# A decoder layer with routed experts: the places of rows in the experts' regions summed by PE, base sums in a buffer of their own, and another order of small parts

## The reference, cut to what matters

```python
x = LN(x + attention(x))            # 8 heads, q/k 64 wide, v 16 wide, relative bias
x = LN(x + mlstm(x, ctx, ctx))      # 4 heads of 32, input and forget gates, decay matrix, running maxima
x = LN(x + ffn(x))

def ffn(x):                                     # H=128, F=512, one shared expert, 8 routed, 2 chosen
    shared = gelu(x @ shared_up) @ shared_down
    probs = softmax(x @ router_w)               # 8 columns
    p, idx = top_k(probs, 2)
    routed = sum over the two chosen e of p_e * (gelu(x @ up[e]) @ down[e])
    return shared + routed + x
```

## Time and profile before

| | us |
|---|---|
| three runs | 477.38, 479.07, 479.12 |
| median | 479.07 |
| profiled execution, its time | 479.12 |
| profiled execution, its span | 477.3 |
| PE busy | 451.4 (95%) |
| PE weight loads busy | 381.6 (80%) |
| DVE busy | 314.0 (66%) |
| ACT busy | 278.6 (58%) |
| POOL busy | 185.4 (39%) |
| mean granted clock of PE | 0.982 |

### The profile page before, as it was taken

One profiled execution on the slowest core, in us unless ns is written; L12 is line 12 of the kernel. 1 busy time (PEld: TensorE's weight loads), 2 busy tenths in 40 slices (PEclk: granted clock), 3 DMA queues, 4 the chain that ended last, 5 costly groups with the idle time before them and its releaser, 6 DMA issues.

```text
span 477.3 us, 15261 instructions
## 1 busy us (share of the span) xinstructions
PE 451.4 (95%) x5178; PEld 381.6 (80%) x5179; DVE 314.0 (66%) x1020; ACT 278.6 (58%) x626; POOL 185.4 (39%) x207
## 2 busy tenths in 40 slices
PE   8899999999988999898799999999999999999994
PEld 6588888888877777666567999999999999999731
DVE  5477888888887478888966666445454444445255
ACT  5678777867685989868768853132233333333236
POOL 5872022102000111117766656477655555554400
PEclk9999999999999999989987999999999999999998
DMA  5341424900000052012211212323222222222196
GB/s 143 87 130 52 103 53 109 237 3 1 3 25 23 25 206 61 25 45 69 63 57 58 74 38 65 90 79 87 75 71 68 66 66 66 66 66 63 47 313 203
DMA packets 47880, 37.98 MB, mean 80 GB/s; under 512 B 5456, under 2 KB 41184, under 8 KB 47824
## 3 DMA queue, kind: packets, MB, share of 16 engines
q1 hardware_dynamic: 43072, 28.10, 21.8%
q0 software_dynamic: 4320, 8.92, 5.2%
q10 hardware_dynamic: 432, 0.20, 0.1%
HBM read 19.30 MB, written 16.34 MB: 75 GB/s over the span
## 4 chain that ended last, share of the span: by engine, by line
PE 59%; DVE 21%; ACT 10%; issue 4%; DMA 4%; DVEq 1%; SPq 0%; POOL 0%; ACTq 0%; POOLq 0%
PE bank L1284 14%; PE bank L1274 14%; PE bank L1234 6%; DMA wdn<-routed 3%; PE bank L966 2%; PE bank L913 2%; PE bank L956 2%; PE bank L915 2%; PE bank L914 2%; DVE negmax L1406 2%; DVE prob L1403 2%; PE pair L1266 2%; DVE tkr L1397 2%; DVE cmat L1504 1%; PE pair L936 1%
## 5 line engine op out<-in xcount | busy, mean ns | idle before, releaser
L853 ACT ACTIVATE prob<-bank 128x512 f32<-128x512 f32 x71 | 42.4, 597 | 104.9 <-PE bank L1274 103.1
L535 POOL DMA_INDIRECT routed<-zbuf x71 | 73.9, 1040 | 59.2 <-DVE zbuf L1763 46.6
L1284 PE MATMUL bank<-wdn,prob 128*128 x568 | 78.2, 281 | 0.2 <-issue 0.2
L1274 PE MATMUL bank<-cT,prob 128*128 128x128 f32 x568 | 76.4, 278 | 0.6 <-DVE cT L1750 0.4
L1274 PEld LDWEIGHTS bank<-cT,prob 128*128 128x128 f32 x568 | 68.9, 191 | 2.3 <-DVE prob L1757 0.8
L1284 PEld LDWEIGHTS bank<-wdn,prob 128*128 128x128 f32 x568 | 68.9, 191 | 1.5 <-issue 0.4
L1757 DVE COPY prob<-wup 128x512 f32 x71 | 30.7, 432 | 45.4 <-PE bank L1274 22.8
L1763 DVE TENSOR_SCALAR zbuf<-bank,zbuf 128x128 f32<-128x128 f32 x71 | 24.9, 351 | 28.6 <-PE bank L1284 28.2
L463 POOL TENSOR_TENSOR hlw<-hst,lnw 128x512 f32<-128x512 f32 x8 | 10.2, 1278 | 72.2 <-ACT hst L745 72.2
L473 POOL DMA_INDIRECT slots<-tkr,slot x32 | 31.8, 995 | 15.1 <-PE bank L1234 5.4
L473 POOL DMA_INDIRECT slots<-zbuf,slot x32 | 31.7, 990 | 13.9 <-PE bank L1234 5.9
(11 more groups left out here) (285 smaller groups left out, 1006.0 us busy)
## 6 DMA issues: line engine op xcount, KB each, us to landing
slots<-x2T SPq DMA_DIRECT2D x8, 585.0 KB, 5.3
zbuf<-slots SPq DMA_DIRECT2D x71, 65.0 KB, 1.9
tkr<-in_x SPq DMA_DIRECT2D x8, 256.0 KB, 3.4
cs<-in_ctx SPq DMA_DIRECT2D x8, 256.0 KB, 2.9
wup<-in_L_ffn_routed_up SPq DMA_DIRECT2D x1, 2048.0 KB, 8.4
zbuf<-tkr SPq DMA_DIRECT2D x8, 256.0 KB
wup<-routed SPq DMA_DIRECT2D x8, 256.0 KB, 3.6
wdn<-routed SPq DMA_DIRECT2D x8, 256.0 KB, 4.4
```

The lines of the kernel that those rows point to most:

```text
L535: pool.indirect_dma_start(routed, bass.IndirectOffsetOnAxis(ap=xr[n][:, :].bitcast(I32)[:, DEST:DEST + 1], axis=0), yr[n % 4][:, :], None) ...
L853: act.activation(hT[:, n % 2, :], bank[2 + n % 2][:, :], ACT.Gelu).then_inc(s["hT_ok"], 1)
L1274: m = mm(bank[2 + n % 2][:, c * P:(c + 1) * P], wst[:, n % 2, c * P:(c + 1) * P], xrT[:, n % 2, :], start=True, stop=True)
L1284: m = mm(bank[6 + n % 2][:, 0:D], hT[:, n % 2, c * P:(c + 1) * P], wdn[:, bass.ds(e * (FC * D) + c * D, D)], start=(c == 0), stop=(c == FC ...
```

## The change

Seven things are done.
1. **Places by PE.** ranks(r) adds up in one PSUM area of 9 x 8 columns (places(r), bank 5 or 6, behind the 264 columns in use): first the running count of each expert region (cum, one row, f32) to all partitions and all nine tiles, then the triangle product, then for each of the 8 tiles its counts to all later tiles. That is ten matmuls in place of two. DVE's rank_out and route_cells go; route_slots reads the places from PSUM and copies one row to cum. ranks moves behind turn_ctx in PE's list.
2. **Base sums** go to total_in, a buffer of their own. base(g) waits for the shared product alone; base(6) stands in front of the loop and base(7) behind the first two turned tiles, instead of behind tile 24.
3. **Choice of experts.** In groups 4 and 6 route_choice stands behind the first score, route_second behind the second, the new parts route_hot and route_gates later; front_rows and residual_b move back one place. Logits of all groups but the last are read behind the normaliser, and in groups 3 and 5 route_logits too; ACT's probabilities stand behind heads_keep of the next group.
4. **High and low parts of x2** for the first two groups come earlier (ACT behind groups 2 and 3, DVE in groups 3 and 5).
5. **Opening:** values(0) behind scores(0,1); POOL's loop of x_lo and bias_in, in this order, ahead of the masks.
6. **Last group of stage A:** residual(7,1) ahead of the gate rows, prob_turn(6,3) ahead of the turns, gates(0) behind heads(7,0), half of rh(0) on POOL.
7. **Scatters:** 7, 6 and 8 in groups 5 to 7 instead of 8 each, 11 instead of 8 in the loop.

```diff
-IN_LOOP = 56
+IN_B = 21
+IN_LOOP = IN_B + 32
...
+    total_in = sb("total_in", [P, NT, D])
...
-    def rank_bank(r):
-        return bank[2 if r < NR - 2 else 6]
+    def places(r):
+        return bank[5 if r < NR - 2 else 6][:, 264:264 + (RT + 1) * E]
...
+        with pool.Fori(1, NG // 2) as i:
+            for n in range(2):
+                x_lo(2 * i + n, n)
+                bias_in(2 * i + n)
...
-        def in_group(g):
-            first = 2 * GT * (g - 5)
+        def in_sixth():
+            weighted(4)
+            pool.wait_ge(s["vc_ps"], 7)
+            scatter(0)
+            pool.wait_ge(s["dd_ps"], GT * 5 + 3)
+            scatter(1)
+            pool.wait_ge(s["u_ps"], GT * 5 + 1)
+            scatter(2)
+            pool.wait_ge(s["dd_ps"], GT * 5 + 4)
+            scatter(3)
+            pool.wait_ge(s["u_ps"], GT * 5 + 2)
+            scatter(4)
+            pool.wait_ge(s["lg_ps"], 4)
+            scatter(5)
+            pool.wait_ge(s["u_ps"], GT * 5 + 4)
+            scatter(6)
...
+        def in_seventh():
+            g, first = 6, 7
+            weighted(g - 1)
+            pool.wait_ge(s["dd_ps"], GT * g + 2)
+            scatter(first)
+            pool.wait_ge(s["vc_ps"], g + 2)
+            scatter(first + 1)
+            pool.wait_ge(s["u_ps"], GT * g + 1)
+            scatter(first + 2)
+            pool.wait_ge(s["dd_ps"], GT * g + 4)
+            scatter(first + 3)
+            pool.wait_ge(s["lg_ps"], g - 1)
+            scatter(first + 4)
+            pool.wait_ge(s["u_ps"], GT * g + 4)
+            scatter(first + 5)
...
+        def in_last():
+            g, first = NG - 1, 13
...
+            weighted(g - 1)
...
-        for g in range(1, NG + 1):
+        pool.wait_ge(s["igsteps"], 4)
+        pool.wait_ge(s["mask_ok"], N_MASK)
+        for h in range(NH // 2, NH):
+            pool.tensor_scalar(rh[0][:, :, h, :], amax[:, :].rearrange("p (a s) -> p a s", a=2),
+                               row[:, NH + h:NH + h + 1], row[:, h:h + 1], ALU.mult, ALU.add).then_inc(s["rh_ok"], 1)
+        for g in range(1, 5):
...
-            if 5 <= g < NG:
-                in_group(g)
-        first = 2 * GT * 3
+        in_sixth()
+        in_seventh()
+        in_last()
+        weighted(NG - 1)
+        first = IN_B
...
             rows_out(t, t % NX)
-            if t % 2 == 0 and IN_LOOP + t // 2 < 2 * NT:
-                scatter(IN_LOOP + t // 2)
+            if t % 3 < 2 and IN_LOOP + t - t // 3 < 2 * NT:
+                scatter(IN_LOOP + t - t // 3)
         with pool.Fori(2, SLOT_TILES // NX) as i:
...
             act.activation(emx[:, :], mrow[:, :], ACT.Exp, scale=emul[:, 0:1]).then_inc(s["emx_ok"], 1)
-            for h in range(NH):
+            for h in range(NH if g > 0 else NH // 2):
                 act.activation(rh[g % 2][:, :, h, :], amax[:, :].rearrange("p (a s) -> p a s", a=2), ACT.Identity,
...
                 heads_keep(g - 1)
+            if g >= 4 and g % 2 == 0:
+                probabilities((g - 4) // 2)
             if now:
...
             group_b(g)
-            if g == NG - 3:
+            if g == 2:
                 x2_high(0)
-            if g == NG - 2:
+            if g == 3:
                 x2_high(1)
...
                 out_turn(g - 1, 2)
+            if not first:
+                prob_turn(g - 1, 3)
             if last:
...
                 turn_x(0)
-            if not first:
-                prob_turn(g - 1, 3)
             if more:
...
             scores(g, 1)
+            if first:
+                pe.wait_ge(s["ld_attn"], 16 * 3)
+                values(0)
             prob_turn(g, 0)
...
                 z_mm(g + 1, 3)
-            if last:
-                pe.wait_ge(s["v_ok"], 2 * NG)
-                gates(0)
             if not first:
...
             heads(g, 0)
+            if last:
+                gates(0)
...
+            if k == 0 and g >= 5 and g % 2 == 1:
+                pe.wait_ge(s["slot_ok"], (g - 3) // 2)
+                pe.wait_ge(s["cum_ok"], (g - 3) // 2)
...
-            if g >= 2:
-                pe.wait_ge(s["rk_ok"], min(g // 2, NR - 2))
...
             pe.wait_ge(s["hotb_ok"], r + 1)
-            if r < NR - 2:
-                pe.wait_ge(s["lg_ok"], 2 * r + 2)
-            else:
+            if r >= NR - 2:
                 pe.wait_ge(s["hsq_ok"], 2 * NG)
-                pe.wait_ge(s["rk_ok"], r)
-            hb = hotb[:, :, :].rearrange("p t e -> p (t e)")
-            mm(rank_bank(r)[:, 0:RT * E], trib[:, :], hb, start=True, stop=True)
-            mm(rank_bank(r)[:, RT * E:2 * RT * E], onesb[:, :], hb, start=True, stop=True).then_inc(s["rank_ps"], 1)
+            if r > 0:
+                pe.wait_ge(s["cum_ok"], r)
+                pe.wait_ge(s["slot_ok"], r)
+            to = places(r)
+            mm(to, one_row[:, :], cum[:, r, :].unsqueeze(1).broadcast_to([1, RT + 1, E]), start=True, stop=False,
+               skip_group_check=True)
+            mm(to[:, 0:RT * E], trib[:, :], hotb[:, :, :].rearrange("p t e -> p (t e)"), start=False, stop=False,
+               skip_group_check=True)
+            for t in range(RT):
+                m = mm(to[:, (t + 1) * E:(RT + 1) * E], onesb[:, :], hotb[:, t, :].unsqueeze(1).broadcast_to([P, RT - t, E]),
+                       start=False, stop=t == RT - 1, skip_group_check=True)
+            m.then_inc(s["rank_ps"], 1)
...
                 centred(g + 1)
-            if g >= 4 and g % 2 == 0:
-                ranks((g - 4) // 2)
             if g == NG - 1:
...
                 turn_ctx(g + 2)
+            if g == 4:
+                pe.wait_ge(s["const_p"], N_TABLES)
+            if g >= 4 and g % 2 == 0:
+                ranks((g - 4) // 2)
             if g == NG - 2:
...
-            mm(bank[FIN_BANK[g]][:, :], ident[:, :], tok[:, g * GT:g * GT + GT, :], start=True, stop=False, skip_group_check=True)
+            mm(bank[FIN_BANK[g]][:, :], ident[:, :], total_in[:, g * GT:g * GT + GT, :], start=True, stop=False, skip_group_check=True)
...
             if last:
+                residual(g, 1)
                 front_rows(0)
...
                 front_keys(0)
-            residual(g, 1)
+            if not last:
+                residual(g, 1)
             assert ast.n == A_STEPS - (1 if first else 0)
...
+
+        def route_hot(b):
             r(tt(hot[:, 1, :, :], cand[:, :, :], spread(m8[:, :], full), ALU.is_equal))
...
+
+        def route_gates(b):
             c = slice(b * RT, b * RT + RT)
...
-        def rank_out(b):
+        def route_slots(b):
             dve.wait_ge(s["rank_ps"], b + 1)
-            dve.tensor_copy(rk[:, :, :, :].rearrange("p k t e -> p (k t e)"), rank_bank(b)[:, 0:2 * RT * E]).then_inc(s["rk_ok"], 1)
-
-        def route_cells(b):
-            dve.wait_ge(s["rk_ok"], b + 1)
-            fl = lambda a: a[:, :, :].rearrange("p e t -> p (e t)")
-            r(dve.tensor_copy(ext[:, :, 1:RT + 1], rk[:, 1, :, :].rearrange("p t e -> p e t")))
-            r(dve.tensor_tensor_scan(fl(cume), fl(segm), fl(ext), 0.0, ALU.mult, ALU.add))
-            r(dve.tensor_copy(ext[:, :, 0], cume[:, :, RT]))
-            r(tt(sl[:, :, :], rk[:, 0, :, :], cume[:, :, 0:RT].rearrange("p e t -> p t e"), ALU.add))
-
-        def route_slots(b):
-            r(tt(sel[:, :, :, :], sl[:, :, :].unsqueeze(1).broadcast_to([P, 2, RT, E]), hot[:, :, :, :], ALU.mult))
+            at = places(b)
+            dve.tensor_copy(cum[:, b + 1, :], at[0:1, RT * E:(RT + 1) * E]).then_inc(s["cum_ok"], 1)
+            r(tt(sel[:, :, :, :], at[:, 0:RT * E].rearrange("p (t e) -> p t e", e=E).unsqueeze(1).broadcast_to([P, 2, RT, E]),
+                 hot[:, :, :, :], ALU.mult))
             dve.tensor_reduce(slot[:, :, b * RT:b * RT + RT], sel[:, :, :, :], AX.X, ALU.max).then_inc(s["slot_ok"], 1)
...
             dve.wait_ge(s["shd_ps"], g + 1)
-            dve.wait_ge(scat[g // 2], 16 * 2 * RT)
-            dve.wait_ge(s["tk_ok"], 16 * (g + 1))
-            tg = tok[:, g * GT:g * GT + GT, :]
-            stt(tg, tg, 2.0, bank[4 + g % 2][:, :].rearrange("p (k d) -> p k d", k=GT),
+            r = slice(g * GT, g * GT + GT)
+            stt(total_in[:, r, :], tok[:, r, :], 2.0, bank[4 + g % 2][:, :].rearrange("p (k d) -> p k d", k=GT),
                 ALU.mult, ALU.add).then_inc(s["base_ok"], 1)
...
             if placed:
-                route_second((g - 4) // 2)
+                route_choice((g - 4) // 2)
             if before:
...
                 x2_out(g - 2)
-            if placed:
-                rank_out((g - 4) // 2)
             if now:
                 score(g, 1)
-            if after:
+            if placed:
+                route_second((g - 4) // 2)
+            if after and not placed:
                 front_rows(g + 1)
...
                 score(g, 2)
+            if placed:
+                route_hot((g - 4) // 2)
+                front_rows(g + 1)
             if after:
                 front_max(g + 1)
-            if before:
```

(51 more changed lines are left out.)

22 lines of the change are left out of this document (6 added, 16 removed).

## The result

The changed kernel took 476.98 us (median of 20 runs, 475.10 to 480.65) against 479.33 for the kernel before (20 runs): ratio 0.9959, 95% interval 0.9942 to 0.9976. Two later comparisons gave 0.9967 (0.9942 to 0.9992) and 0.9964 (0.9943 to 0.9985). The ratios put the change at 1.6 to 2.0 us, the differences of the medians at 1.4 to 2.4; forecast were 2.6 (476.5). Ratios leave out executions that took over 1.5% longer than the fastest of the same kernel.

A forecast was written before the change was run, and what follows sets the result against it. PE bounds the shared expert and expert loop, DVE's list stage B, a DVE-ACT-PE cycle stage A. Terms -0.8 -0.15 -1.0 -0.7 -0.85 +1.2 -0.3 sum to -2.6: 479.12 to 476.5 us; own range 475.0 to 478.2, overall 473.6 to 479.8.

The forecast's parts named there:

- Opening, -0.8: Start of stage A: values(0) behind scores(0,1) brings the first scores and heads earlier, -0.8 us (ends 0, -1.07).
- Last group of stage A, -0.15: End of stage A: reordering removes PE's wait before the last heads, but only -0.15 us is won (ends +0.4, -1.2).
- Placed groups, -1.0: Stage B, groups 4 and 6: a shorter DVE list saves 0.5 us in each, -1.0 in all.
- between nrm and cmat, -0.7: Stage B, after groups 3 and 5: this stretch falls to 1.27 us each, saving 0.14 and 0.59, -0.7 together.
- POOL's block: Groups 4 and 6: DVE's delay behind POOL's hlw product, half taken as gone, -0.25 us each (ends 0, -0.5).
- Group 7, -0.85: End of stage B: qk(7,2) comes right behind cmat, so ACT's wait before the table load goes, -0.85 us (ends 0, -0.85).
- Rival 2: Stage B: ACT replaces DVE's list as bound, so none of -1.0, -0.7 and -0.85 comes; 479.0 us, chance 0.12.
- Shared stage, +1.2: ranks(2) and ranks(3) in PE's full list: ten matmuls cost 0.65 us a call, +1.2 in all (ends +0.6, +3.8).
- Expert loop, -0.3: Loop: base(6) and base(7) leave it, so the PE blocks behind them get shorter, -0.3 us (ends 0, -0.5).
- POOL's backlog: Loop, first 16 tiles: POOL falls 3 us behind with its scatters and catches up; zero cost, if not, 1 to 3 us.
- a sign of being wrong: PE waiting between group 1's first shared product and the loop's end would show the forecast wrong; no size given.
- Rivals 1 and 4: PE's low clock: 1, gone before the dense stretch, 474.1 us, chance 0.15; 4, one more spell in PE-bound stretch, 478.2, 0.13.

The follow-up runs named there:

- e2_values: Changed kernel with values(0) put back before the last z product; 477.92 us, ratio 0.9985 to the kernel before.
- e5_dve: Changed kernel's order and buffers, but DVE sums the places again; 496.49 us on another chip, ratio 1.0040 to the kernel before.
- e6_choice: Changed kernel with the choice of experts back at its old place in groups 3 and 5; 497.80 us on another chip, ratio 1.0068 to the kernel before.
- f1_decay: Changed kernel with each group's first decay ahead of the copy of the heads on ACT; 477.24 us, ratio 0.9951 to the kernel before.
- f2_decays: As f1_decay, plus the second decay right behind the heads copy and its cmat ahead of the variance; 477.96 us, ratio 0.9950 to the kernel before.
- c0_changed: The changed kernel run again without edits; the two such repeats took 477.30 us (ratio 0.9967 to the kernel before) and 477.67 us (0.9964).
- f3_all: f2_decays with bias_in(0) held until wq_lo is whole and 9 scatters, not 11, in the loop's first 16 tiles; 476.73 us, ratio 0.9944 to the kernel before.
- e4_twice: Changed kernel with the ten place-summing matmuls issued twice in both shared-stage calls; 479.53 us, ratio 1.0012 to the kernel before.
- e3_bias: Changed kernel with POOL's bias_in(0) waiting until wq_lo is whole; 493.81 us on another chip, ratio 0.9989 to the kernel before.

## Why the prediction was right, point by point

- *Opening, -0.8:* -0.73 from z to the first output, and it reaches stage B. The first scores were at 17.80, not 16.75, because of the race for z.
- *Last group of stage A, -0.15:* the wait before the last heads went, and PE waited 1.31 before o(7,3) instead, as the text had it. What is left of the gain over stage A, 0.25, is this term (see e2_values).
- *Placed groups, -1.0, and between nrm and cmat, -0.7:* after groups 3 and 5 `cmat` came 1.25 behind the last part of `nrm` (forecast 1.27). From `nrm` to `nrm` group 4 gained 0.67 (15.08 to 14.41), group 6 1.44, group 5 0.16: 2.3 against 1.7. The surplus is in groups 5 and 6; the kernel before had low spells in groups 4 and 6 (the latter running on into the earlier trace rows), and how much they took is not shown. That the shorter list counts is shown by e5_dve. The term that was off the other way is POOL's block: half was to go; 0.54 and 0.55 stayed of 0.72 and 0.80, where 0.22 is free, so two fifths went.
- The Trainium skill (SBUF — State Buffer, section Who interferes with whom) says that such pairs exclude each other. The 1.15 against 0.22 and the 2.42 against 1.43 agree: an instruction moved next to POOL's is not helped, only its phase to POOL's start counts.
- *Group 7, -0.85:* -0.96, the table load directly behind the third decay. But this may be luck. The kernel before has one profile, and in it PE ran at 1.2 GHz until 241.3 (not until 243.3, as the prediction has it; the shared products that ended there took 0.39 each, full speed):

```profile
238.45 1.12 PE L1120 MATMUL bank<-qblk,cT 128*64 128x256 f32 x4
```

  The four strings from there to the first shared product took 3.27, in the changed kernel at full clock 1.88. ACT's wait of 0.84 is shorter than these 1.4, so it could have gone with the spell alone. In e6_choice, where the clock stayed low until 0.6 into group 7, 0.26 of the wait was there in the new order too:

```profile
243.71 0.38 ACT L774 ACTIVATE decay<-bank 128x256 f32<-128x256 f32 x1 [0.26 <-PE bank L1161]
```

  No profile of the kernel before without a spell there is on record, so the two are not told apart.
- *Rival 2* (ACT is the bound of stage B) is out as it stands, since DVE's list counted in e5_dve. By the waits in e6_choice and f1_decay, though, ACT is close behind: what DVE saves further comes back as waits for ACT.
- *Shared stage, +1.2:* +1.15 where both have a spell there (52.97 against 51.82; it lasted until 4.7 behind that `nrm` before, until 4.8 to 5.9 in the two of the changed kernel), 0.62 to 0.70 a call. The first changed profile shows 0.4 less than before only because it had no spell. What the text missed is the use of the sum on PE for this stage: e5_dve shows DVE's cells would make PE wait 1.6 there in this order.
- *Expert loop, -0.3:* **wrong, the step that failed**, while the total lay near the forecast. From the first to the last turn before took 137.38, the six profiles of the changed code with 11 scatters (without f2_decays, 137.6 too) 137.6 to 138.6, +0.2 to +1.2 in place of -0.3. The term for base's leaving, -0.3, is what was wrong: it won nothing that shows. Tile 24, behind which it stood (2.41), takes 2.59 to 2.73 in five of six profiles without it and 2.06 in one, for in its place PE waits 0.33 to 0.35 for DVE's copy of the weights, which takes 0.66 there and 0.43 elsewhere:

```profile
350.57 1.13 PE L1323 MATMUL bank<-cT,prob 128*128 128x128 f32 x8 [0.35 <-DVE prob L1801]
```

  And the last turn comes 2.15 behind the one before it, not 1.90, which is all of the +0.2 that every profile of the changed code on these chips has at least. Why the copy and the last turn are longer is open; base's move had no experiment of its own. "Zero; if not, 1 to 3" for POOL's backlog is 0.8 at most. PE did wait in this stretch, which the prediction had named as a sign of being wrong.
- *Rivals 1 and 4* are chance on either side: of 14 profiles (before, changed, experiments) two had no spell between 150 and 300, the others one to four, from 3.4 to 14 us long, at 0 to 4 us each. Rival 1's mark, no low clock in front of the dense stretch, was there in the first changed profile, and the two others show that it was chance. Over the 12 runs of c0_changed 475.10 went with a mean clock of 0.993 and 479.46 with 0.983, but 475.36 with 0.984: the clock is a part of the spread of some 5 us between runs of one kernel, and not all of it (the start of z, and a stall in stage A that stands at the end, are others). That spells come and go between executions of one kernel agrees with the rule of the Trainium skill cited in the prediction (TensorE: Matmul & The Clock Gate, section What's actually happening).

By parts: -0.75 -0.25 -3.3 +1.15 and +0.2 to +1.2 for the loop make -2.0 to -3.0; the three ratios say -1.6 to -2.0. The difference has the size of what group 7 may owe to the spell. So the mechanism of the opening, of the placed groups and of the shared stage is borne out, each by an experiment that undid or doubled it (for the order of the choice with low spells beside it); the closeness of the sum is in part luck, since stage B's surplus of 0.8 on one profile of the kernel before stands against the loop's miss of 0.5 to 1.5. Items 2, 4, 6 and 7 of the change were not undone singly, but for the scatters of the loop.

## What to carry to other kernels

Where one list bounds a stage, a summation of a few hundred cells is cheap on PE (0.65 us for ten matmuls) and dear on DVE (1.5), and its relief may show one stage later as well. Moving work into an engine's free time pays only until the next engine in the ring is full: here DVE's savings beyond the change came back as waits for ACT. When a profile differs by a microsecond, look in a second one of the same code before giving it a cause, and of the kernel before too: here a term of the forecast was read beside a low spell that other profiles do not have.

## What was not expected of the hardware

- Adding bf16 matmuls (128 rows, 8 to 64 columns) into the same cells start 0.03 apart; the whole string 0.62 to 0.68.
- Low clock spells of 14 us in stage B (f1_decay 228 to 242, e2_values 229 to 243), with which group 7 took 16.2 and 15.9 us in place of 12.2 (f3_all had one from 202 to 216, in groups 4 and 5); one in stage A (135 to 139) cost 1.3.
- On one chip the first 20 tiles of the loop took some 15 us more, with long gaps on PE, ACT and DVE together. Before many of them the profile shows no releaser: the engine waited for nothing that it records. The cause is open.
- In e4_twice stage A took 2.2 us more over two outputs near 90 us, at full clock, in code that was not touched; it began with PE idle for 0.84 between two matmuls of one z product, with no releaser. f2_decays lost 1.4 at the same place. Open.
- In e3_bias group 7 took 13.26 in place of 12.19 without a wait of the kinds above. Open.
